# Rotary cross-attention in steps of two: two key projections, then scores, weighing, scores, weighing, with the next context turned right behind the values

## What is computed

```python
lat, ctx = layer_norm(latents), layer_norm(context)      # each with gain and shift
q = (lat @ Wq).reshape(b, n, 16, 64)
k, v = split(ctx @ Wkv)                                   # 16 heads of 64 each
k = apply_rope(k, cos, sin)          # x1*cos - x2*sin, x2*cos + x1*sin on the halves of a head
attn = softmax(clip(q @ k.T * 64 ** -0.5, -11, 11))       # over 2048 positions
out = (attn @ v) @ Wo + bo
```

## Time and profile before

| | |
|---|---|
| median of 3 runs | 1168.32 us (1167.96 to 1169.67) |
| the profiled execution, its own time | 1169.31 us |
| its span, first to last instruction | 1167.5 us |
| mean granted TensorE clock | 0.997 |
| PE busy, of the span | 1144.4 us, 98% |
| PEld busy | 946.2 us, 81% |
| DVE busy | 804.8 us, 69% |
| ACT busy | 547.2 us, 47% |
| POOL busy | 268.0 us, 23% |
| rotary stage, first projection to last weighing | 28 to 511 us of the span |

### The profile page before, as it was taken

The page is one execution under the profiler, slowest core; times in us unless marked ns, Lnnn a source line. Parts: engine busy times, 40 slices in busy tenths (PEclk is TensorE's granted clock), DMA queues, the critical chain, the costliest instruction groups (busy, mean ns, idle before and its releaser), DMA issues.

```text
span 1167.5 us, 23727 instructions
## 1 busy us (share of the span) xinstructions
PE 1144.4 (98%) x9856; PEld 946.2 (81%) x9856; DVE 804.8 (69%) x1363; ACT 547.2 (47%) x900; POOL 268.0 (23%) x226
## 2 busy tenths in 40 slices
PE   8999999999999999999899999999999999999998
PEld 6778888788788888855457777988899999999997
DVE  7868595959695959466788884475665655665563
ACT  6343434333434333124379996584544445444451
POOL 0144353534352626240153520010000000000000
PEclk9999999999999999999999999999999999999999
DMA  9233232323232314345123317302544545445440
GB/s 359 89 118 118 82 118 75 127 73 127 73 128 71 129 37 137 119 180 217 73 73 146 118 70 286 145 1 111 214 182 180 215 151 210 182 177 215 151 174 19
DMA packets 37377, 159.62 MB, mean 137 GB/s; under 512 B 3739, under 2 KB 3995, under 8 KB 26788
## 3 DMA queue, kind: packets, MB, share of 16 engines
q1 hardware_dynamic: 37284, 158.29, 36.8%
HBM read 153.56 MB, written 4.72 MB: 136 GB/s over the span
## 4 chain that ended last, share of the span: by engine, by line
PE 49%; DVE 2%; issue 2%; ACT 2%; DVEq 0%
PE mid_bk L57 11%; PE mid_bk L58 11%; PE mid_bk L59 11%; PE mid_bk L1284 5%; PE mid_bk L1299 2%; PE mid_bk L1254 2%; PE mid_bk L1162 2%; PE mid_bk L1329 1%; PE mid_bk L1319 1%; PE mid_bk L1443 0%; ACT sa_sc L1608 0%; DVE x_sc L1901 0%; PE mid_bk L1393 0%; PE mid_bk L1382 0%; PE mid_bk L1217 0%
## 5 line engine op out<-in xcount | busy, mean ns | idle before, releaser
L668 POOL TENSOR_TENSOR norm_both<-norm_both,prob 128x512 f32<-128x512 f32 x118 | 163.8, 1389 | 88.0 <-DVE prob L425 80.6
L58 PE MATMUL mid_bk<-mo_x_lo,mo_w_hi 128*128 128x256 f32 x496 | 141.1, 284 | 0.0
L59 PE MATMUL mid_bk<-mo_x_hi,mo_w_lo 128*128 128x256 f32 x496 | 141.0, 284 | 0.0
L57 PE MATMUL mid_bk<-mo_x_hi,mo_w_hi 128*128 128x256 f32 x496 | 141.0, 284 | 0.0
L592 ACT ACTIVATE prob<-u_ps 128x512 f32<-128x512 f32 x128 | 66.1, 604 | 141.9 <-PE u_ps L798 141.9
L1997 DVE TENSOR_TENSOR mo_w_lo<-w_raw,mo_w_hi 128x2048 fp32r<-128x2048 f32 x32 | 73.3, 2292 | 72.7 <-ACT mo_w_hi L1698 72.7
L57 PE MATMUL k_ps<-ctx_hi,wk_hi 128*128 128x512 f32 x256 | 102.5, 400 | 1.1 <-DVE turned L405 1.1
L1698 ACT ACTIVATE mo_w_hi<-w_raw 128x2048 fp32r<-128x2048 f32 x32 | 61.2, 1913 | 87.7 <-PE mid_bk L59 87.7
L57 PE MATMUL mid_bk<-mo_w_hi,mo_h_hi 128*128 128x512 f32 x256 | 100.2, 391 | 0.0
L58 PE MATMUL k_ps<-ctx_lo,wk_hi 128*128 128x512 f32 x256 | 100.2, 391 | 0.0
L58 PE MATMUL mid_bk<-mo_w_lo,mo_h_hi 128*128 128x512 f32 x256 | 99.9, 390 | 0.0
(11 more groups left out here) (295 smaller groups left out, 2503.8 us busy)
## 6 DMA issues: line engine op xcount, KB each, us to landing
w_raw<-in_w SPq DMA_DIRECT2D x64, 1024.0 KB, 6.1
wk_hi<-wk_parts SPq DMA_DIRECT2D x28, 512.0 KB, 4.1
wk_lo<-wk_parts SPq DMA_DIRECT2D x28, 512.0 KB, 5.2
ctx_raw<-in_ctx_rows SPq DMA_DIRECT2D x8, 1024.0 KB, 5.6
x_k<-in_ctx_T SPq DMA_DIRECT2D x8, 1024.0 KB, 7.2
x_val<-in_ctx_heads SPq DMA_DIRECT2D x8, 1024.0 KB, 5.2
tabs<-in_rot_tabs SPq DMA_DIRECT2D x8, 512.0 KB, 4.0
vals<-in_wq_rows SPq DMA_DIRECT2D x4, 512.0 KB, 9.5
```

Of the source, the lines that this page charges most:

```text
L57: pe.matmul(out, w_hi, x_hi, start=start, stop=False)
L58: pe.matmul(out, w_hi, x_lo, start=False, stop=False)
L59: return pe.matmul(out, w_lo, x_hi, start=False, stop=stop)
L668: ins = pool.tensor_tensor(to, to, src, ALU.add)
```

## The change

TensorE's list now goes in pairs of steps, t even: project(t, 0), values(n, 1) and transposes(n + 1) if r = 2, project(t, 1), project(t + 1, 0), project(t + 1, 1), scores(t - 1), weigh(t - 2), scores(t), weigh(t - 1), and values(n, 0) if r = 0. No matmul is added or taken away. ACT's eight `context` instructions come two steps' places earlier, behind `keep_products(n, 1)` and ahead of exponent(4n + 1), and the waits that guard the shared banks follow. DVE's list changes at one place: center(1) goes ahead of turn_second(2). POOL's and SP's lists stay as they are.

```diff
@@ DVE, once
             add_products(0, 1)
+            center(dve, 1)
             turn_second(2)
             low_k(3)
-            center(dve, 1)
@@ ACT, in the loop over t
-                if t < NT and r == 3 and n + 1 < NC:
-                    for k in range(KD):
-                        context(n + 1, k, k)
...
                 if t < NT and r == 2:
                     keep_products(n, 1)
+                    if n + 1 < NC:
+                        for k in range(KD):
+                            context(n + 1, k, k)
                 if t >= 1:
                     exponent(t - 1)
@@ PE, transposes(n, k, bank)
-                    pe.wait_ge(s["exped"], 4 * (4 * n - 3) + bank + 1)
+                    pe.wait_ge(s["v_sum"], 10 * n)
+                    pe.wait_ge(s["v_kept"], 4 * n)
@@ PE, scores(t)
-                if t % 4 == 2 and n + 1 < NC:
+                if t % 4 == 1 and n + 1 < NC:
                     pe.wait_ge(s["cfull"], 4 * (n + 1) + 4)
@@ PE, the order
-            for t in range(NT + 1):
+            project(0, 0)
+            project(0, 1)
+            project(1, 0)
+            project(1, 1)
+            scores(0)
+            values(0, 0)
+            for t in range(2, NT, 2):
                 n, r = t // 4, t % 4
+                project(t, 0)
...
+                if r == 2:
+                    values(n, 1)
+                    if n + 1 < NC:
                         for k in range(KD):
                             transposes(n + 1, k, k)
...
+                project(t, 1)
+                project(t + 1, 0)
+                project(t + 1, 1)
+                scores(t - 1)
+                weigh(t - 2)
+                scores(t)
+                weigh(t - 1)
+                if r == 0:
                     values(n, 0)
+            scores(NT - 1)
+            weigh(NT - 2)
```

More of the change, by code:

```diff
@@ L865, in _ @@
             queries(3)
-            for t in range(NT + 1):
-                n, r = t // 4, t % 4
-                if t < NT:
-                    if r == 3 and n + 1 < NC:
+            project(0, 0)
[5 more added lines that the diff above has]
+            for t in range(2, NT, 2):
+                n, r = t // 4, t % 4
+                project(t, 0)
+                if t == 18:
+                    pe.wait_ge(s["v_sum"], 5 * 9)
+                    denominators(0)
+                if r == 2:
+                    values(n, 1)
+                    if n + 1 < NC:
                         for k in range(KD):
                             transposes(n + 1, k, k)
[L872 to L883, removed]
+                project(t, 1)
[6 more added lines that the diff above has]
+                if r == 0:
                     values(n, 0)
+            scores(NT - 1)
+            weigh(NT - 2)
             pe.wait_ge(s["rope"], 6 * NT)
```

## The result

| | before | after |
|---|---|---|
| median | 1168.32 us (1167.96 to 1169.67, 4 runs) | 1224.12 us (1222.04 to 1229.27, 4 runs) |
| ratio, 95% interval | | 1.0475 [1.0447, 1.0503] |
| the profiled execution | 1169.31 us, span 1167.5 | 1222.04 us, span 1220.3 |
| mean granted TensorE clock | 0.997 | 0.984 |

Slower by 4.8%. The forecast was 1212.8 us in a range of 1198 to 1224, so the direction and the places were right and the size was 11 us short; the median lies at the very end of the range, 0.1 us above it.

A forecast was written before the change was run, and what follows sets the result against it. TensorE was taken as full in the rotary stage, so idle terms add: -3.0 + 6.0 + 7.1 + 5.2 + 29.0 + 1.2 = 45.5, taken as +44.5 on 1169.3, less 1.0: 1212.8 us, range 1198 to 1224.

The forecast's parts named there:

- the 3.0 us for the visits: One visit to the tiles per pair instead of two, 0.20 us each for 15 pairs: a gain of 3.0 us.
- Term 1: The second scores of a pair wait for the exponents, 2.30 us from weighing instead of 1.90: 15 x 0.40 = +6.0 us.
- Term 2: Transposes behind the values wait for the last addition: 1.0 us in six chunks, +6.0, and +1.1 for chunk 1.
- Term 3: project(3, 0) waits for DVE's low_k(3), with one to three instructions lengthened by POOL: +5.2 us.
- Term 4: project(4n + 5, 0) waits for DVE's turn_first(4n + 4), 3.1 us seven times, more in two places: +29.0 us in all.
- stays hidden behind DVE's 16.8: At project(4n + 5, 0), wk_lo lands at 15.5 us, before DVE's turn ends at 16.8, if landing takes within 6.4.
- the test that I had set: The prediction is wrong if L57 waits for the DMA of wk_lo more than for DVE.
- Term 5: At the stage's end scores(31) waits for turn_second(31), now behind clip(29): +1.2 us.
- The clock is 1.00 in the chunk, so nothing is to be had there: In a whole chunk of the rotary stage TensorE's granted clock is already 1.00, leaving nothing to win.
- The short chain: Rival: POOL's additions miss DVE's turn and sums, 9.67 us loses three times 1.07; 1194 us, chance 0.12.
- The loads: Rival: wk_lo takes 8 us to land and holds project(4n + 5, 0): 1223 us; chance 0.10, shared with longer blocking.
- The rule of the Trainium skill: DVE and GpSimd share an exclusive lock, so contested DVE instructions could lose up to 1.6 us, not 1.09: 1224 us.

The follow-up runs named there:

- e8: The paired kernel with its other obstacles moved (loads, sums, low_k(3), later layers' instructions), but transposes again directly behind values(n, 1): 1193.83 us, ratio 1.0196.
- e1: The changed kernel with the weights of the next step ahead of the tables in SP's queue: 1223.36 us, ratio 1.0448.
- e5: The changed kernel with 12 useless matmuls in front of project(4n + 5, 0) in seven chunks and of project(3, 0): 1212.98 us, ratio 1.037.
- e4: One part of the change alone: step-by-step order of the kernel before, with transposes directly behind the values: 1186.34 us, ratio 1.0145.
- e7: The changed kernel with weights loaded ahead of tables and POOL's additions of step 4n + 1 held back until clip(4n + 2): 1209.2 us, ratio 1.0329.
- e9: Pairs kept, obstacles moved, transposes behind project(t, 1), plus first two sums ahead of turn_first(4n + 4) and clip(4n + 2) behind it: 1199.47 us, ratio 1.0257.
- e10: The kernel before with only center(1) moved ahead of turn_second(2) in DVE's list: 1167.42 us, ratio 0.9991.

## Why the prediction was right in kind and short in size

- **The bound and the ceiling.** Right. TensorE was full, so every wait counted, and the 3.0 us for the visits could not show against them; no run tests this term alone.
- **Term 1, the second scores.** Right to the hundredth: fifteen waits of 0.33, from weighing to scores 2.30 us as in the earlier trace rows.
- **Term 2, the transposes.** 5.0 us by the list, six times 0.83; with the start of the first transpose 1.0 each, as forecast, and 2.8 for chunk 1. e8 confirms it alone.
- **Term 3, low_k(3).** Oversized: 3.7 us measured, 5.2 taken. That is the price without any instruction lengthened by POOL (3.8 in the sum); I had reckoned with one to three of them.
- **Term 4, project(4n + 5, 0).** The place and the count were right; the sum was 29.0 and the waits are 13.5 + 10.5 - 1.1 = 22.9. Half of the 6.1 us is step 21: 3.8 forecast, 0.8 measured. DVE was as late there as forecast, but the 24 matmuls in front ran slowly behind the wait of step 20 and filled the time:

```profile
363.42 0.77 PE L57 MATMUL k_ps<-ctx_hi,wk_hi 128*128 128x512 f32 x1 [4.11 <-DVE turned L405]
...
372.75 0.47 PE L57 MATMUL k_ps<-ctx_hi,wk_hi 128*128 128x512 f32 x1 [0.82 <-DVE turned L405]
```

 The two lie 9.3 us apart; at 0.227 us the 24 matmuls take 5.4 of them, so the wait would have been 3.9. The other half is 2.0 us in the five plain chunks, 0.9 in step 13 and 0.2 in step 20. Two steps were off here. The piece from turn_second to the next turn_first takes 165.75 - 156.76 = 8.99 us and not 9.67, since fewer instructions are lengthened beside POOL's additions: one of the sums, not two. And the sentence that the load "stays hidden behind DVE's 16.8" failed: wk_lo takes a median of 5.9 us to land here, not 5.2, and is later than the turn in five chunks of seven. By the test that I had set, L57 waiting longer for the DMA (13.5) than for DVE's turn (10.5), this step was wrong. It cost the number little, because in four of these five chunks the two limits lie within half a microsecond (e1; in step 5 they are 1.6 us apart).
- **Term 5.** 1.3 at scores(31), 1.0 net of the old 0.3; forecast 1.2.
- **What was missing.** The terms as measured give -3.0 + 6.0 + 6.9 + 3.7 + 22.9 + 1.0 = 37.5 us, and the stage lost 53.2. The step that failed is "The clock is 1.00 in the chunk, so nothing is to be had there": true of what could be won, and I never asked what could be lost. In the changed kernel 60 distances between matmul starts in the stage are 0.40 to 0.44 us long instead of 0.227, together 12 us (the kernel before has one). They stand behind waits: of the eight of 2.5 us and more at L57, seven are followed by such distances (that of step 25, 2.6 us, is not). 3 of the 12 us are no loss, since they only shortened the wait of step 21. So the lowered clock cost 53.2 - 37.5 - 3.0 = 12.7 us. e5 fills the gaps and gives 11.1 us back; e4, whose waits are all 1.6 us or less but for one of 2.8 (after which the clock stayed full there), has a clock of 0.998 and comes out at its sum. Some 4 of the 12.7 us lie outside these distances and are not followed further; the transposes of chunk 1, for one, take 2.76 us instead of 1.97.
- **The rivals.** The short chain did not come by itself, but e7 makes it: there these instructions are 2.5 us shorter in a chunk (the rival had 3.2), and the time is 1209, not 1194. The loads came last by little, with some 6 us to landing and not the 8 of that rival. The rule of the Trainium skill, "SBUF — State Buffer", section "SBUF: two separate sides", would have given 1224, near the measured number, but not for its reason: the contested instruction takes 1.76 us here, an extra of 1.08, as before. That the two engines get in each other's way e7 bears out; that the lock is exclusive, as that page says, no run here shows.

## What to carry to other kernels

An in-order engine that serves two others is a chain: before work is regrouped on the full engine, walk the list of the other one from its first late wait to the result that is needed next, and do the same for the DMA queue, because a limit that lies 1.3 us below the other in the sum, as the load did here, may come out above it. Where a full engine gets gaps of some microseconds, look at its granted clock behind them: here the lowered clock cost 11 to 13 us on top of some 40 us of waits. And an edit that gives 1 us alone and another that gives 3, neither clear of noise, may give 20 together; try them together before either is dropped.

## What the runs showed of the hardware that was not expected

- Waits of 2.5 to 4.5 us on TensorE, which had run almost without a pause before, were followed by stretches at half clock (0.50 and 0.52 in the two windows above), in most places but not in all. In e1 five waits of 2.1 to 2.2 us were too, in e9 only three of the seven waits of 2.4 to 2.7 us in front of the scores. So the length of a wait alone does not tell whether the clock falls behind it. The Trainium skill, "TensorE: Matmul & The Clock Gate", section "Part 1: The HAM clock gate (the "warmup" mystery)", names 1.2 GHz as the clock of the idle state and 2.4 GHz as that of the busy one; the distances of 0.43 and 0.227 us fit these two levels.
- Useless matmuls in the gaps made the kernel 11.1 us faster (e5).
- Runs of one kernel differ with the granted clock: in e10 the mean clock goes from 0.991 to 0.999 and the time from 1172.02 to about 1166.5 us.
